# Order of VectorE and GpSimd around a closing rotation, width of the reciprocals' transfers, and the steps of the first layer's outputs

## The reference

```python
# layer 0: heads of 64, inner width 1024
h = layernorm(x) * gamma + beta
Q, K, V = h @ Wq, context @ Wk, context @ Wv
attn = softmax(einsum('bihd,bjhd->bhij', Q, K)) * 64 ** -0.5
x = x + einsum('bhij,bjhd->bihd', attn, V) @ Wo + bo
# layer 1: heads of 32, inner width 512
q = rmsnorm(x) * norm_w @ wq;  k, v = split(context @ wkv)
q, k = unit_length(rotate(q)), unit_length(rotate(k))
attn = softmax(einsum('bqhd,bkhd->bhqk', q, k) * 32 ** 0.5)
out = x + einsum('bhqk,bkhd->bqhd', attn, v) @ wout
```

## Time and profile before

| | |
|---|---|
| median of 3 runs | 3159.71 us (3157.25 to 3162.65) |
| span of the profiled execution, first to last instruction | 3155.9 us |
| TensorE busy | 3038.5 us, 96% |
| VectorE busy | 2275.2 us, 72% |
| ScalarE busy | 1395.2 us, 44% |
| GpSimd busy | 532.1 us, 17% |
| mean granted TensorE clock | 0.997 |

### The profile page before, as it was taken

How to read it: one execution, slowest core, us unless ns; L and a number is a source line. 1 busy time by engine, 2 the same in 40 slices (tenths; PEclk the granted TensorE clock), 3 DMA queues, 4 the chain that set the end, 5 groups by cost and what they waited for, 6 DMA issues and landing times.

```text
span 3155.9 us, 70590 instructions
## 1 busy us (share of the span) xinstructions
PE 3038.5 (96%) x30408; PEld 1484.1 (47%) x30408; DVE 2275.2 (72%) x2555; ACT 1395.2 (44%) x1497; POOL 532.1 (17%) x349
## 2 busy tenths in 40 slices
PE   7999998999999999999999999999999999999998
PEld 4444444554444444555344444455544444445553
DVE  4777776787677767678667777768866777776867
ACT  3333333566433333355643333345563333334555
POOL 1000003460100001344010000125401000012540
PEclk9999999999999999999999999999999999999999
DMA  3010000111110101020120011001112010100001
GB/s 119 19 27 22 26 22 20 59 28 39 54 48 22 27 22 27 16 63 22 42 76 23 22 26 26 26 17 59 28 36 79 22 26 22 27 22 20 22 17 39
DMA packets 178445, 107.13 MB, mean 34 GB/s; under 512 B 81501, under 2 KB 147165, under 8 KB 178137
## 3 DMA queue, kind: packets, MB, share of 16 engines
q1 hardware_dynamic: 178136, 102.60, 12.0%
HBM read 93.12 MB, written 9.42 MB: 32 GB/s over the span
## 4 chain that ended last, share of the span: by engine, by line
PE 83%; DVE 8%; issue 3%; ACT 3%; DMA 2%; POOL 1%; SPq 0%; DVEq 0%; ACTq 0%
PE o_acc L722 19%; PE scores L710 18%; PE work L749 13%; PE work L743 12%; PE work L794 10%; PE work L669 5%; DVE acc L903 3%; PE work L781 3%; ACT probs L830 1%; DVE tile_max L885 1%; PE work L775 1%; PE scores L703 1%; PE work L785 1%; DVE stats L920 1%; DMA rows_dram<-recip_t 1%
## 5 line engine op out<-in xcount | busy, mean ns | idle before, releaser
L830 ACT ACTIVATE probs<-scores 128x1024 f32<-128x1024 f32 (+1 forms) x744 | 934.2, 1291 | 446.0 <-PE scores L710 438.1
L885 DVE TENSOR_REDUCE tile_max<-work 128x2 f32<-128x1024 f32 x500 | 611.5, 1223 | 437.0 <-PE work L669 436.8
L903 DVE TENSOR_TENSOR acc<-acc,probs 128x1024 f32<-128x1024 f32 (+1 forms) x544 | 858.6, 1578 | 30.8 <-ACT probs L830 6.9
L722 PE MATMUL o_acc<-probs,v_tok 128*64 128x512 f32 (+1 forms) x4096 | 769.3, 605 | 0.0
L794 PE MATMUL work<-wo,o_sum 128*32 128x512 f32 (+1 forms) x2072 | 398.5, 598 | 34.6 <-issue 21.5
L710 PE MATMUL scores<-q_high,k_high 64*128 64x512 f32 (+1 forms) x1952 | 369.7, 491 | 0.8 <-ACT probs L830 0.8
L1030 POOL CAST neg_max<-neg 128x8 bf16<-128x8 f32 x64 | 24.1, 377 | 1736.9 <-DVE neg L890 1736.9
L722 PEld LDWEIGHTS o_acc<-probs,v_tok 128*64 128x64 f32 (+1 forms) x4096 | 164.4, 122 | 324.2 <-issue 315.3
L987 DVE TENSOR_TENSOR resid<-work,resid 128x512 f32<-128x512 f32 x384 | 261.6, 685 | 67.5 <-PE work L794 67.3
L669 PE MATMUL work<-k_high,q_high 64*128 64x512 f32 x1000 | 268.0, 531 | 31.7 <-DVE tile_max L885 22.4
L710 PE MATMUL scores<-q_low,k_high 64*128 64x512 f32 (+1 forms) x1952 | 297.3, 391 | 0.0
(11 more groups left out here) (89 smaller groups left out, 2744.9 us busy)
## 6 DMA issues: line engine op xcount, KB each, us to landing
recip<-rows_dram SPq DMA_DIRECT2D x380, 64.0 KB, 2.1
stage<-in_x_dram SPq DMA_DIRECT2D x8, 1024.0 KB, 7.5
wq<-in_L_xattn_Wq_dram SPq DMA_DIRECT2D x32, 256.0 KB, 2.8
resid<-in_x_dram SPq DMA_DIRECT2D x8, 1024.0 KB, 5.2
wo<-in_L_xattn_Wo_dram SPq DMA_DIRECT2D x32, 256.0 KB, 2.7
out_dram<-resid SPq DMA_DIRECT2D x7, 1024.0 KB, 4.3
wk<-in_L_xattn_Wk_dram SPq DMA_DIRECT2D x32, 192.0 KB, 2.5
wv<-in_L_xattn_Wv_dram SPq DMA_DIRECT2D x32, 192.0 KB, 2.5
```

The costliest lines, as they stand in the source:

```text
L722: mm = pe.matmul(o_acc[h * d:(h + 1) * d, :], v_tok[par][:, kt, h * d:(h + 1) * d], probs[:, unit_slot(t, n, kt, h // 2), h % 2, :], start ...
L830: act.activation(block_probs(t, n, kt), scores[:, 2 * (no % 2):2 * (no % 2) + g, :], ACT.Exp, scale=(1.0, float(D1) ** 0.5 / QK_SCALE ** 2 ...
L885: dve.tensor_reduce(tile_max[:, qt, :, n:n + 1], maxima_banks(e), AX.X, ALU.max, negate=True).then_inc(dve_freed, 1)
L903: dve.tensor_tensor(a, block_probs(t, n, 0) if kt == 1 else a, block_probs(t, n, kt), ALU.add).then_inc(add_ok, units)
```

## The change

Three edits. First, `on_vector`: where `rest` stands in a step whose fill ends in `kr` or `qr`, VectorE and GpSimd now take it ahead of that rotation (this happens in steps 1 and 2 of (7,0) alone); and in a step of layer 0 whose fill has an output, `norm_o` now comes behind the first maximum, no longer ahead of it. Second, SyncE spreads reciprocals by as many transfers as the turn has heads, each as wide as a head: two of 64 partitions in layer 0, four of 32 in layer 1 as before; the count that VectorE waits for follows. Third, for all halves of layer 0 but (7,0) the four outputs move one step later: output 0 into step 3, outputs 1, 2 and 3 into steps 0, 1 and 2 of the half after.

```diff
@@ add_results
-        beside[2][:0] = outs[0:1]
-        beside[3][:0] = outs[1:2]
+        beside[3][:0] = outs[0:1]
@@ make_plan
-                for i in range(2):
-                    beside[i] = E("out", t0, n0 * HT + 2 + i) + beside[i]
+                for i in range(HT - 1):
+                    beside[i] = E("out", t0, n0 * HT + 1 + i) + beside[i]
@@ on_vector
-    ahead = norm + st.first + [e for e in st.early if e.kind != "norm_o"]
+    if any(e.kind == "out" for e in st.fill) and st.t is not None and TURN[st.t][1] == 0:
+        ahead = st.first + norm + [e for e in st.early if e.kind != "norm_o"]
+    else:
+        ahead = norm + st.first + [e for e in st.early if e.kind != "norm_o"]
     at = max([n for n, e in enumerate(st.fill) if e.kind in WORK], default=0)
-    if st.rest and st.fill and st.fill[at].kind in HIGHS:
+    if st.rest and st.fill and st.fill[at].kind in HIGHS + ("kr", "qr"):
         return ahead, st.fill[:at] + st.rest + st.fill[at:]
@@ 
+def recips_after(t, n):
+
+    return sum(HEADS_OF[u] for u, _ in HALVES[:half_no(t, n)])
@@ send_recips
-                g, no = HEADS_OF[t], half_no(t, n)
+                g, d, no = HEADS_OF[t], WIDTH_OF[t], half_no(t, n)
...
-                for h in range(G1):
-                    row = h * g // G1
-                    sp.dma_start(recip[h * D1:(h + 1) * D1, :], rows[1, row:row + 1, tokens(n)].to_broadcast([D1, HALF])).then_inc(recip_in, 16)
+                for h in range(g):
+                    sp.dma_start(recip[h * d:(h + 1) * d, :], rows[1, h:h + 1, tokens(n)].to_broadcast([d, HALF])).then_inc(recip_in, 16)
@@ normalize_sums
-                dve.wait_ge(recip_in, 16 * G1 * half_no(t, n))
+                dve.wait_ge(recip_in, 16 * recips_after(t, n))
```

## The result

The changed kernel took 3139.29 us, median of 4 runs (3134.94 to 3141.18); the kernel before, run beside it, 3160.13 (3157.25 to 3162.65). The ratio is 0.9927, 95% interval 0.9912 to 0.9941: faster by 20.8 us, where 23.7 were forecast (3136 us). In a second comparison it took 3139.48 against 3163.78, ratio 0.9926 [0.9912, 0.9941], 24.3 us. The profiled execution took 3138.32 us at a granted clock of 0.996 (before: 0.997), and its span is 19.5 us shorter. Lines of the kernel before stand six lines further down in the changed kernel: L669 is L675 there.

What follows compares the result with a forecast made beforehand. TensorE was taken to bound the kernel, with 117.4 us idle. The terms 14.4 + 5.7 + 3.2 + 0.8 - 0.4 = 23.7 us gave 3136 us, range 3127 to 3147.

Steps and rivals of the forecast that it cites:

- What bounds the kernel: Whole kernel: TensorE, busy 3038.5 of 3155.9 us, sets the time; reordering can give at most its 117.4 us idle.
- Edit 1a: Steps 1 and 2 of (7,0): last maximum ahead of the rotation saves 3.6 of 7.0 us a batch, 14.4 in all.
- Edit 1b: Step 2 of halves (1,0) to (6,0): norm behind the first maximum saves 0.13 us in 44 halves, 5.7 in all.
- The doubt whether the 0.13 was the shapes': Common step 2s: the 0.13 us might come from the change of shapes, not the bank; then nothing is gained.
- The loss in (0,0): (0,0) of batches 1 to 3: norm behind the maximum lengthens the chain, losing 0.13 x 3 = 0.4 us.
- Edit 2: Step 2 of (6,1): two spreading transfers, 128 KB landing in 2.3 us, complete the row about 0.65 us earlier.
- Edit 3: Outputs one step later: 3.2 us over four batches in (6,1), 0.8 us over four at layer 1's start.
- layer 1's start: Last output of (7,1) goes into step 2 of layer 1: 0.2 us gained a batch, 0.8 over four.
- Contention: Rival: GpSimd's rotation falls beside maxima, adds in (7,0) run at 2.54 instead of 3.20 us; 3125 us, chance 0.13.
- Only the rotation pays: Rival: 0.13 belongs to the shapes, (7,0) gives its lower 12.8, layer 1 loses 2.7; 3149 us, chance 0.16.
- No effect: Rival: waits in (7,0) are only moved; time stays within 6 us of 3160, chance 0.05.
- Slower: Rival: 64-partition transfer lands so late that the norm holds VectorE in some 52 halves; near 3168 us, chance 0.04.

Runs made afterwards that it cites:

- the shift first: The kernel of the closing output, with the shift's transposition ahead of the three outputs in step 2 of (6,1): 3127.04 us, ratio 0.9887.
- the short rotation: Changed kernel with GpSimd's addition and multiplication for layer 1's first key rotation cut to 32 of 512 elements a partition, output wrong: 3125.92 us, ratio 0.9879.
- the norm ahead: Changed kernel with the old line for `ahead`, so the norm stands ahead of the first maximum everywhere: 3146.74 us, ratio 0.9944.
- the kernel of the closing output: Changed kernel where VectorE in layer 0 also takes the step's last maximum ahead of an output that ends the fill: 3136.54 us, ratio 0.9909.

## Why the prediction was right, and which terms were not

**What bounds the kernel** held: TensorE's busy time stayed (4.1 us of 3038.5 less) and its waits paid.

**Edit 1a**, 3.6 us a batch: measured 23.43 - 19.88 = 3.55, and alone 14.1 us in the medians (14.4 forecast). The pieces came as worked out: adds of 3.43 (3.2 to 3.6), a new wait of 0.63 for the output's bank (0.4 to 0.9), 2.53 us at (6,1) (2.4). The 0.76 before the output is not named in the forecast, but its time is: 478.4, and it came at 476.42, with everything 1.98 earlier than before. Only the second pair, 3.45, was above its 3.0 to 3.4. It is VectorE's sum that decides, so 3.9 of the 7.0 us of waits stayed under other names. The Trainium skill's remark ("GPSIMD Engine Reference", Key points) that GpSimd contends with VectorE's two-input instructions in SBUF agrees with 3.43 against 2.54.

**Edit 1b**, 0.13 us in 44 halves: half by half 0.11 to 0.15 nearly everywhere, the chain's output at 0.86, and 5.4 to 7.3 us when it is undone. The doubt whether the 0.13 was the shapes' is answered: it was the bank. The loss in (0,0) was 0.21 to 0.23 in three batches, not 0.13: 0.6 instead of 0.4 us.

**Edit 2**, 0.65 us earlier in (6,1): the step that failed. I put 128 KB between 64 and 192 KB at 2.3 us. It landed in 3.0, an issue took 0.55 us and not 0.43, and together that eats the two issues saved; TensorE's wait for the norm, which was to go, is 0.29. The estimate went by bytes; the 192 KB row is a load of a weight matrix, another shape of transfer, and what made this one slower was not taken apart. The Trainium skill's fixed 2.0 us and 436 GB/s ("DMA: Bandwidth & Descriptors", Anatomy of one DMA — SWDGE (gpsimd) path), a fit for transfers that GpSimd issues, gave an estimate of 2.3 too. These are issued by SyncE and measured 3.0; the measurement decides.

**Edit 3**: in (6,1) 0.8 a batch was forecast. From the denominators' product to step 3's first scores it was 16.04 us in the mean of four batches before and is 16.48 with an output of 0.86 more in it: 0.42 gained, but between -0.3 and 1.4 in the single batches, so this term is the least certain. The reciprocals come no earlier, and three additions in a row (1.88 us) hold the transposition of the shift, 1.08 us; before, it was 0.86 in front of the rotation's. The run with the shift first gets 0.76 of this back. At layer 1's start 0.2 a batch was forecast and TensorE's wait fell by 0.82. I had added the output's 0.68 to VectorE's chain whole. That was mis-sized: from the start of the two adds to the end of the norm it is 576.54 - 569.51 = 7.03 us before and 572.92 - 565.86 = 7.06 after, with the addition in it. The first add takes 2.28 in both. The output's addition falls beside GpSimd and still takes its usual 0.68; the second add and the norm start later against GpSimd's two operations (by 0.39 and 0.28 us, measured from the first add) and take 2.78 and 0.68 instead of 3.16 and 0.93. So VectorE's chain grows by next to nothing, and nearly the whole 0.86 that TensorE is earlier comes off its wait.

**The sum** with these sizes: 4 x (3.55 + 1.45 + 0.82 + 0.42) - 0.6 = 24.4 us, against 20.8 and 24.3 in the two comparisons and 19.5 in the one pair of spans. The pair of spans has 4.1 us more at the lower clock after than before (last section), about 2 us of time. The forecast's 23.7 is as near by luck in part: two errors of opposite sign, 1.5 too much in (6,1) and 2.5 too little in layer 1.

**The rivals.** Contention didn't go; the short rotation shows that it would have been worth about 7 us. Only the rotation pays: refuted by the 10.9 us without it. No effect: the stretch got 3.55 us shorter a batch, and 3.11 of its 7.03 us of waits did go. Slower: no norm of a common half of layer 0 waits for its row of 3.0 us. In (7,1) VectorE waits 3 to 5 us for it, with four transfers as with two.

## What to carry to other kernels

When an engine's own sum of work is what decides, a better order on it moves the waits rather than removes them: work out that sum, forecast what stays, and then look for what makes its pieces longer. Here that was GpSimd's two-input work beside VectorE's adds; making GpSimd wait until the adds are done let it finish 0.9 us later, which nothing waited for, and gained 6 to 7 us by the halves (12 by the ratios, with a higher granted clock). Test edits of a schedule singly and in pairs: the norm behind the maximum loses 12 us alone and gains 5 to 7 with the outputs moved. And list the granted clock of every run beside its time: here, by the estimate, it accounts for 4 to 6 us of differences that the halves don't show.

## What the runs showed of the hardware

A read of one row of 2 KB from HBM into 64 partitions (128 KB) lands in 3.0 us at an issue of 0.55; into 32 partitions (64 KB) in 2.0 to 2.1 at 0.43. Contention goes both ways and by more than either row alone had shown: GpSimd's addition of 128x512 takes 1.28 us with no add beside it and 2.30 beside adds, its multiplication 1.05 and 1.91, a pair of VectorE's adds 2.54 and 3.43.

The rows read as if the two engines took turns. VectorE's first add (476.88) ends at 478.10 in its usual 1.22. GpSimd's addition, which began 0.06 after it, ends at 479.23, 1.13 later (1.28 without adds). The second add ends at 480.31, 1.08 after that (1.22 undisturbed), and GpSimd's multiplication at 481.22, 0.91 after that (1.05). In all four batches and in every kernel here with this order the first add takes 1.21 or 1.22 and the second 2.11 or 2.12. So the pair loses 0.9 us, about one GpSimd operation that gets in between its two adds, and GpSimd's two operations lose 1.9 us in all, in which they wait for adds. That they take turns is read from these times; no run was made to test it. Operations that take one of their inputs from PSUM, the additions of an output, stay at 0.68 beside GpSimd.

TensorE's granted clock falls to its lower level, 1.2 GHz, for short stretches that differ from kernel to kernel and are not in the same places: 23.5 us in all in the kernel before, 27.6 in the changed one, 20.4 in the short rotation's, 45.2 with the norm ahead. Two windows, one of the kernel before and one of the changed kernel (length, busy time of PE, PEld, DVE, ACT, POOL, then the granted clock):

```profile
2041.20:2044.60 3.40, 3.40 (x49) 3.40 (x46) 0.00 (x0) 0.60 (x1) 0.00 (x0) 0.66 0.02 5
```

```profile
525.60:529.00 3.40, 2.39 (x16) 2.06 (x18) 0.96 (x3) 1.37 (x2) 3.40 (x2) 0.71 0.02 5
```

The first comes right after (7,0)'s waits of 1.80 and 2.31 us in batch 2; in the second TensorE had worked through (9.64 of the 10.6 us ahead at a clock of 1.00) until a wait of 1.98 that ends inside it. A half that holds one more such stretch is some 1.6 us longer: (7,1) of the kernel of the closing output takes 37.73 us in batch 0, with one, and 36.06 in the three others, without. So a single span says less than the medians about a change of 5 us; it is one reason why spans, medians and sums of rows differ here by 3 to 5 us. Of these stretches five begin in (7,0), (6,1) and (7,1) in the kernel before, six in each of the changed kernel's two profiles, three with the closing output, and one or two in the short rotation's and where GpSimd waits; but nine with the norm or the outputs moved alone, whose (7,0) is nearly that of the kernel before. What sets their number stays open.
